# Four graph layers in one kernel: later layers' loads spread out, rank-4 rows last in a score stage, and new order plans

## The reference

```python
# layer 0: 8 heads of width 32, mask, output projection, layer norm
scores = where(adj + eye > 0, q @ k.T / sqrt(32), -inf);  out = softmax(scores) @ v
x = layernorm(x + out @ Wo.T + bo) * gamma + beta
# layer 1: 8 heads, scores + a_i + c_j + log(adj + 1e-9), then x + out
# layer 2: one head: softmax(leaky_relu(q_i + k_j + (1 - adj) * -1e9)) @ (x @ W_fc) + x
# layer 3: as layer 0, with + log(max(adj, 1e-8)) in place of the mask
```

## Time and profile before

| | |
|---|---|
| median of 3 runs | 1794.17 us (1792.88 to 1796.88) |
| profiled execution: its time, its span | 1796.79 us, 1795.0 us |
| mean granted TensorE clock | 0.991 |
| busy share PE, PE weight loads, DVE, ACT, POOL | 94%, 72%, 76%, 67%, 74% |
| HBM read and written | 62.93 MB, 8.39 MB |

### The profile page before, as it was taken

One profiled execution on the slowest core, in us unless ns is written; L12 is line 12 of the kernel. 1 busy time (PEld: TensorE's weight loads), 2 busy tenths in 40 slices (PEclk: granted clock), 3 DMA queues, 4 the chain that ended last, 5 costly groups with the idle time before them and its releaser, 6 DMA issues.

```text
span 1795.0 us, 53987 instructions
## 1 busy us (share of the span) xinstructions
PE 1684.0 (94%) x23308; PEld 1290.8 (72%) x23308; DVE 1371.3 (76%) x2556; ACT 1203.0 (67%) x1886; POOL 1330.2 (74%) x994
## 2 busy tenths in 40 slices
PE   4899999899999999889999999989999999998996
PEld 3677776787776777677777677767777777766874
DVE  2899777767699976776779987776778998777674
ACT  2567875467877786456877787546687778754675
POOL 3555799278977499638987759945898767992788
PEclk8999999999999999999999999999999999999998
DMA  7100010102121001100222100010123200101001
GB/s 217 43 19 19 16 29 25 36 14 66 55 89 49 18 15 37 31 19 19 74 82 66 37 19 20 27 47 7 31 73 94 61 19 14 32 25 36 14 26 42
DMA packets 76432, 74.79 MB, mean 42 GB/s; under 512 B 6562, under 2 KB 76196, under 8 KB 76196
## 3 DMA queue, kind: packets, MB, share of 16 engines
q1 hardware_dynamic: 75092, 70.55, 13.2%
q10 hardware_dynamic: 1104, 0.79, 0.1%
HBM read 62.93 MB, written 8.39 MB: 40 GB/s over the span
## 4 chain that ended last, share of the span: by engine, by line
PE 78%; DVE 9%; POOL 5%; ACT 3%; issue 3%; SPq 2%; DMA 1%; DVEq 0%; POOLq 0%; ACTq 0%
PE gx L640 23%; PE sc L738 18%; PE od L780 17%; PE gx L792 6%; PE sc L744 3%; PE sc L732 3%; PE gx L828 3%; PE gx L665 2%; ACT ring L906 1%; DVE negm L999 1%; PE gx L758 1%; DVE xs L1088 1%; DVE lg L1070 1%; DVE parts L999 1%; POOL xs L632 1%
## 5 line engine op out<-in xcount | busy, mean ns | idle before, releaser
L625 POOL TENSOR_TENSOR ring<-ring,adj_c 128x1024 f32<-128x1024 f32 x256 | 605.4, 2397 | 11.1 <-ACT ring L906 8.7
L738 PE MATMUL sc<-qk 32*128 32x256 f32 x9216 | 410.5, 294 | 31.2 <-DVE negm L999 11.1
L738 PEld LDWEIGHTS sc<-qk 32*128 32x128 f32 x9216 | 320.5, 184 | 135.6 <-issue 76.2
L888 ACT ACTIVATE aside<-sc 128x1024 f32<-128x1024 f32 x192 | 196.7, 1024 | 166.2 <-PE sc L738 113.3
L906 ACT ACTIVATE ring<-sc 128x1024 f32<-128x1024 f32 x256 | 248.3, 1023 | 49.9 <-PE sc L744 49.4
L780 PE MATMUL od<-ring,vf 128*32 128x256 f32 x3072 | 243.3, 388 | 7.0 <-issue 5.0
L780 PE MATMUL od<-ring,halves 128*32 128x256 f32 x3072 | 237.3, 380 | 0.0
L999 DVE TENSOR_REDUCE parts<-sc 128x4 f32<-128x1024 f32 x128 | 156.6, 1223 | 98.3 <-PE sc L738 96.8
L598 POOL TENSOR_TENSOR xs<-xs,bo 128x512 f32<-128x512 f32 x96 | 128.8, 1342 | 120.5 <-DVE xt_lo L969 120.1
L1026 DVE TENSOR_TENSOR ring<-ring,adj_c 128x1024 f32<-128x1024 f32 x128 | 182.2, 1464 | 0.0
L1002 DVE TENSOR_REDUCE parts<-aside 128x4 f32<-128x1024 f32 x128 | 154.9, 1211 | 16.7 <-ACT aside L888 16.5
(11 more groups left out here) (144 smaller groups left out, 4231.2 us busy)
## 6 DMA issues: line engine op xcount, KB each, us to landing
adj_c<-in_adj_t SPq DMA_DIRECT2D x96, 256.0 KB, 2.8
adj_r<-in_adj SPq DMA_DIRECT2D x64, 256.0 KB, 3.0
x_raw<-in_x_t SPq DMA_DIRECT2D x32, 256.0 KB, 3.4
xs<-in_x SPq DMA_DIRECT2D x32, 256.0 KB, 3.3
out<-xs SPq DMA_DIRECT2D x32, 256.0 KB, 2.2
wo<-in_w_o SPq DMA_DIRECT2D x2, 256.0 KB
ring<-in_w_q ACTq DMA_DIRECT2D x1, 256.0 KB, 3.8
ring<-in_w_k ACTq DMA_DIRECT2D x1, 256.0 KB, 5.1
```

The lines of the kernel that those rows point to most:

```text
L625: pool.tensor_tensor(part, part, adj_c[i.mi % 3][:, t, :].unsqueeze(1).to_broadcast([P, G, N]), ALU.mult).then_inc(weighted, 1)
L738: mm = pe.matmul(sc[:, g, t * N:(t + 1) * N], buf[rows, a, c, t * P:(t + 1) * P], buf[rows, b, c, :], start=(n == 0 and not masked), stop= ...
L888: act.activation(aside[:], sc[:, 0:2, :], ACT.Copy).then_inc(set_aside, 1)
```

## The change

Five things are changed.

1. At the start SP issues adj of item 1 early, adj transposed of item 0 ahead of x, and x of items 0 and 1 alone. The other loads of the first group go where their LX, LR and LC stages stand in SP's order. The 14 small transfers and the 7 weights go a few at a time behind LR.3 to LR.7. SPLIT_AT moves the splits of these weights later.
2. In a half of S or E, the 24 products of both blocks t come first, and the 8 products of `m_rows` or `c_rows` last. The wait for these rows moves behind the 24 products. Only the first product of a bank has the start flag.
3. In layer 0's S, the mask products wait only for the mask, and the wait for q and k comes behind them.
4. On POOL, the scaling of q's bias moves from ahead of the loop to behind T.0; the scaling of the biases of layers 1 and 3 moves from PC.5 to PC.7.
5. All plan places and the pitches are new numbers.

```diff
-SPLIT_AT = (None, -0.06, -0.05, 13, 15.2, 17.4, 19.6, 21.8, 24, 26.2)
+SPLIT_AT = (None, -0.06, -0.05, 19, 21, 23, 27, 33, 37, 41)
...
-    "S": {PE: [5.649, 6.16], ACTE: [6.962, 8.435], DVE: [6.511, 7.353]},
+    "S": {PE: [3.017, 5.338], ACTE: [5.417, 6.963], DVE: [4.727, 6.83]},
...
-    "A": {PE: [14.601, 15.151, 16.002, 16.487]},
+    "A": {PE: [13.593, 15.277, 15.581, 15.629]},
...
-    "E": {PE: [9.469, 11.767], ACTE: [11.406, 12.866], POOL: [1.816, 2.912], DVE: [12.575, 16.68]},
-    "A": {PE: [15.565, 15.586, 16.838, 16.969]},
+    "E": {PE: [8.072, 10.461], ACTE: [10.807, 12.327], POOL: [-6.299, -5.344], DVE: [2.323, 5.591]},
+    "A": {PE: [13.92, 14.286, 15.186, 15.196]},
...
-PITCH = {0: (4.4, 4.65), 1: (4.55, 4.45), 2: (4.65, 4.4), 3: (4.9, 4.95)}
+PITCH = {0: (4.6, 4.65), 1: (4.55, 4.55), 2: (4.75, 4.7), 3: (4.95, 4.9)}
...
+            sp.dma_start(adj_r[1][:], adj_all[rows_of[1].batch]).then_inc(adjr_loaded[1], 16)
             for dst, src in fold_plain:
                 sp.dma_start(dst, src).then_inc(w_fold, 16)
-            for i in items_l0[:GROUP]:
+            sp.dma_start(adj_c[0][:], adj_t_all[mha[0].batch]).then_inc(adjc_loaded[0], 16)
+            for i in items_l0[:2]:
                 sp.dma_start(xs[:, i.slot], x_all[i.batch]).then_inc(x_loaded[i.slot], 16)
...
-            for dst, src in plain:
-                sp.dma_start(dst, src).then_inc(w_plain, 16)
-            for n in range(3, len(WEIGHTS)):
-                load_weight(n)
+            def some_later_loads(n):
+                for dst, src in plain[6 * n:6 * n + 6]:
+                    sp.dma_start(dst, src).then_inc(w_plain, 16)
+                if n >= 2:
+                    for m in range(3, len(WEIGHTS))[3 * (n - 2):3 * (n - 1)]:
+                        load_weight(m)
...
+                    if 3 <= i.ar < GROUP:
+                        some_later_loads(i.ar - 3)
...
-            pool.wait_ge(w_first, 32)
-            pool.tensor_scalar(b_col["q0"][:], b_col["q0"][:], SCALE, None, ALU.mult).then_inc(cols_set, 1)
...
+                    if i.k == 0:
+                        pool.wait_ge(w_first, 32)
+                        pool.tensor_scalar(b_col["q0"][:], b_col["q0"][:], SCALE, None, ALU.mult).then_inc(cols_set, 1)
...
-                    if c == 0:
-                        if s == "S":
-                            pe.wait_ge(qk_lo_set, 4 * i.mi + 4)
-                            if i.l == 0:
-                                pe.wait_ge(mask_r_set, i.i0 + 1)
-                            if i.l == 1:
-                                pe.wait_ge(c_set, i.i1 + 1)
-                        else:
-                            pe.wait_ge(m_set, i.mi + 1)
...
-                        if extra is not None:
+                    if extra is not None:
+
+                        if c == 0:
+                            if s == "S":
+                                pe.wait_ge(c_set, i.i1 + 1)
+                            else:
+                                pe.wait_ge(m_set, i.mi + 1)
+                        for t in range(T):
                             for g in range(G):
```

More of the change, by code:

```diff
@@ L72 @@
-    "A": {PE: [14.601, 15.151, 16.002, 16.487]},
[L73 to L78, removed]
+    "O": {PE: [1.438], ACTE: [3.649], POOL: [-5.383]},
+    "T": {PE: [-4.035], ACTE: [-2.229], DVE: [-2.359]},
+    "Q": {PE: [-1.726], ACTE: [0.972], DVE: [0.299]},
+    "P": {PE: [-1.297], ACTE: [1.062], DVE: [0.516]},
+    "V": {PE: [0.406], ACTE: [2.076], DVE: [96.525]},
+    "S": {PE: [3.017, 5.338], ACTE: [5.417, 6.963], DVE: [4.727, 6.83]},
@@ L79 @@
+    "U": {DVE: [7.669]},
+    "M": {PE: [6.711], ACTE: [9.416]},
+    "E": {PE: [9.03, 10.762], ACTE: [10.388, 13.272], POOL: [4.746, 6.815], DVE: [15.191, 18.748]},
+    "A": {PE: [13.593, 15.277, 15.581, 15.629]},
+    "N": {DVE: [17.555]},
+    "F": {PE: [19.617]},
+    "XB": {POOL: [-7.724]},
+    "H": {DVE: [20.491]},
+    "LC": {SP: [44.42]},
+    "PC": {POOL: [-2.071]},
 }
 MHA_PLAN3 = {
-    "T": {PE: [-6.128], ACTE: [-5.034], DVE: [-6.002]},
-    "Q": {PE: [-0.869], ACTE: [0.837], DVE: [-0.372]},
@@ L94 @@
-    "LC": {SP: [22.274]},
-    "PC": {POOL: [-8.955]},
+    "T": {PE: [-6.107], ACTE: [-3.304], DVE: [-4.058]},
+    "Q": {PE: [-2.126], ACTE: [0.858], DVE: [0.342]},
+    "P": {PE: [0.592], ACTE: [1.918], DVE: [1.811]},
+    "V": {PE: [0.99], ACTE: [3.205], DVE: [63.745]},
+    "S": {PE: [2.413, 5.408], ACTE: [5.042, 6.794], DVE: [3.811, 6.542]},
+    "U": {DVE: [7.247]},
+    "M": {PE: [7.245], ACTE: [9.928]},
+    "E": {PE: [8.072, 10.461], ACTE: [10.807, 12.327], POOL: [-6.299, -5.344], DVE: [2.323, 5.591]},
@@ L96 @@
+    "A": {PE: [13.92, 14.286, 15.186, 15.196]},
+    "N": {DVE: [18.138]},
+    "F": {PE: [22.254]},
+    "XB": {POOL: [-17.948]},
+    "H": {DVE: [24.89]},
+    "LC": {SP: [24.223]},
+    "PC": {POOL: [-15.21]},
 }
 LN_PLAN0 = {
-    "B": {DVE: [23.449]},
-    "Z": {ACTE: [27.077]},
-    "Y": {DVE: [26.124], ACTE: [29.319], POOL: [27.197]},
+    "B": {DVE: [23.655]},
+    "Z": {ACTE: [26.241]},
+    "Y": {DVE: [26.25], ACTE: [27.932], POOL: [21.459]},
 }
 LN_PLAN3 = {
-    "B": {DVE: [27.746]},
@@ L104 @@
-    "Z": {ACTE: [31.23]},
-    "Y": {DVE: [30.39], ACTE: [34.223], POOL: [24.809]},
+    "B": {DVE: [25.008]},
+    "Z": {ACTE: [29.699]},
+    "Y": {DVE: [29.765], ACTE: [31.356], POOL: [17.541]},
 }
 FIRST_PLAN = {
[L108 to L111, removed]
+    "LT": {SP: [12.581]},
+    "LX": {SP: [33.723]},
+    "LR": {SP: [16.812]},
+    "PR": {POOL: [-19.152]},
 }
 LAST_PLAN = {
-    "OUT": {SP: [61.449]},
+    "OUT": {SP: [62.32]},
@@ L115 @@
 }
 GAT_PLAN = {
[L117 to L124, removed]
-    "LR": {SP: [29.847]},
-    "PR": {POOL: [-7.166]},
+    "T": {PE: [-6.852], ACTE: [-4.101], DVE: [-4.465]},
+    "G": {PE: [-3.965, -0.755], DVE: [-2.968, 1.37]},
+    "J": {ACTE: [1.804]},
@@ L127 @@
+    "K": {PE: [5.971]},
+    "L": {DVE: [8.022]},
+    "X": {ACTE: [11.185]},
+    "W": {PE: [11.789], ACTE: [14.078]},
+    "C": {DVE: [15.008], PE: [12.88]},
+    "LR": {SP: [28.845]},
+    "PR": {POOL: [-11.907]},
 }
-PITCH = {0: (4.4, 4.65), 1: (4.55, 4.45), 2: (4.65, 4.4), 3: (4.9, 4.95)}
+PITCH = {0: (4.6, 4.65), 1: (4.55, 4.55), 2: (4.75, 4.7), 3: (4.95, 4.9)}
 GAT_START, LAST_START = 23, 31
```

96 lines of the change are left out of this document (42 added, 54 removed).

## The result

The changed kernel takes 1787.87 us (median of 9 runs, 1784.17 to 1791.53), the kernel before 1795.74 us beside it. The ratio is 0.9963, 95% interval 0.9952 to 0.9973: faster by some 0.4%, 6 us slower than forecast. Against the kernel before beside it, it gains 7.9 us; 12.2 were forecast (1794.17 to 1782). The profiled execution has a time of 1789.48 us and a span of 1787.4 us.

A forecast was written before the change was run, and what follows sets the result against it. PE, busy 94% of the span, was taken as the bound, with about 125 us of waits. From 1796.8: -18.5 - 2 - 0.6 + 3.7 + 5 = 1784.4; the median is 2.6 lower: 1782 us, range 1764 to 1798.

The forecast's parts named there:

- The start, -18.5: First layer's start: E0.0 would start at 32.4 us in place of 50.94, saving 18.5 us, bounds -14 to -20.5.
- a wait inside the stage breaks the stream: Rival, chance 0.04: row products in E0 and S0 pay 0.1 us behind each wait, 13 us in all, giving 1795.
- The spread splits, -2: DVE from 60 to 100 us: weight splits spread over twice the stretch save 2 us, between 0 and -4.
- The clock at the start: New start stays at 2.4 GHz; if not, P.1 and S1.0 take 1.3 and 1.2 us more, losing 2.5.
- The body, +6.1: Everything behind the start: PE's new order -0.6, waits for `sc` +3.7, waits for `gx` +5, spread splits -2.
- +3.7 for `sc`: PE's waits for the single buffer `sc` between S and E halves, summed over layers 1, 3 and 0: +3.7 us.
- +5 for `gx`: PE's waits for the two `gx` buffers, almost all in layer 2: 37 to 42 us, so +5.
- Layer 1's term: More work between S1 and E1 in layer 1: waits for `sc` go from 15.2 to 3.7 us, -11.5.
- Layer 3's was +8.6: Less work between E1 and S0 in layer 3: waits for `sc` go from 8.7 to 17.3 us, +8.6.
- Layer 0's was +6.7: S and E halves next to each other in layer 0: waits for `sc` go from 2.9 to 9.6 us, +6.7.
- POOL sets layer 3's pace: Rival, chance 0.16: in layer 3, A3 waits for POOL, 1 us in 24 items, giving 1806 us.
- The body gains as well: Rival, chance 0.22: layer 1's 11.5 us come, layer 3's 8.6 and half the `gx` term go, giving 1768 us.

The follow-up runs named there:

- start_only: The kernel before with only the start's part of the change (SP's order, SPLIT_AT, POOL's bias steps): 1777.75 us, ratio 0.9903; again 1779.54 us.
- early_x: The kernel before with only x transposed of items 2 and 3 issued earlier on SP, ahead of the small loads and later weights: 1777.51 us, ratio 0.9901.
- rows_last_only: The kernel before with only the new form of a score stage, parts 2 and 3 of the change: 1793.92 us, ratio 0.9991.
- new_plans_old_stage: The changed kernel with the old form of a score stage, all waits first: 1789.20 us, ratio 0.9966.
- start_old_splits: start_only with the later weights' splits and POOL's scaling of the later biases back at their old places: 1776.83 us, ratio 0.9900.
- early_y: The changed kernel with Y.32, Y.64 and Y.96 on POOL moved ahead of PC and XB, PE's order unchanged: 1775.82 us, ratio 0.9887; again 1773.61 us.
- both: early_y with T.40, T.72 and T.104 also placed 0.6 units later on PE, ACT and DVE: 1777.71 us, ratio 0.9892.
- late_t: The changed kernel with T of layer 1's first slot 0.6 units later on PE, ACT and DVE in every group: 1777.33 us, ratio 0.9902.

## Why the prediction was partly wrong

**The start, -18.5: right.** E0.0 at 32.85 (forecast 32.4), behind `pick`; start_only, the spread splits among it, gives 17.6 us. The cause was narrower than the change: one late load (early_x).

**Rows last and mask first, 0: right** (rows_last_only, new_plans_old_stage). The rival that a wait inside the stage breaks the stream is refuted.

**The spread splits, -2: wrong**, no gain (start_old_splits). The busy share of one window, 60 to 100 us, said that the splits are in the way there; it did not say that they are less so further on.

**The clock at the start: right for P.1 and S1.0.** From 18 to 30.5 us the granted clock is 1.00, as the sum had it, and PE did not idle there. That is also what the Trainium skill's "TensorE: Matmul & The Clock Gate", section "Why this matters for your kernels", has: it is the long idle gap between bursts that puts PE back to half clock. The sum left out what comes next: PE idles 2.35 us ahead of E0.0, and from 32.8 to 37.0 us the clock is 0.57 to 0.61, which makes the 0.91 of the window. E0.0 to E1.0 takes 7.46 us in place of 6.63 before, so 0.8 us. That wait alone does not decide it: behind the same wait (2.36 and 2.34 us) early_y and both kept 1.00, late_t fell to 0.61 to 0.63.

**The body, +6.1 (-0.6 + 3.7 + 5 - 2): this is the step that failed**: it took every input of a stage as ready, so the wait of T for POOL's layer norm stood at nothing. It failed twice, in opposite directions. From E1.0 to E1.127 the body takes 9.4 us more than before (40.3 to 1761.5, in place of 57.6 to 1769.4). early_y's body takes 16.4 us less than the changed kernel's (39.2 to 1744.0), so 7.0 less than before's:

- *Left out:* the wait of T.40, T.72 and T.104 for Y on POOL, +16.4 us in these profiles, +12 to +14 by the medians. I had counted only what each pair of neighbours on PE shares, `sc` and `gx`, and taken each input as ready. The one input that comes down the other engines from the layer before was not: T.40 would have started 1.5 us after P.39 in place of 6.1, and its input was there after 5.1. 10.6 us of it are in the list of waits, 5.4 are the slower stretches behind them (below).
- *Over-priced:* the terms of +3.7 for `sc` and +5 for `gx`, where the cured order gives -7.0 in these profiles and -2 to -6 by the medians of the two pairs. Some 5 of the 7.0 lie behind E1.71, in stretches in which two runs of the old order differ by as much as 2.3 us (286.2 and 283.9 from E1.103 on, in before and rows_last_only); by a whole group, E1.39 to E1.71, it is -0.1, where the terms make +2. Layer 1's term was -11.5; seven items took 1.5 us less, which is 7 us for the layer's 32. The list of waits has 11.1 us of them before and 3.6 after, where the sum had 15.2 and 3.7. Layer 3's was +8.6, and the wait came: M to S0 takes 0.3 us more per item, 2.1 of the 2.8 us by which seven items grew (after the change one more pair of A2 and A3 lies in that stretch, 1.7 us, and other stages give 1 back). The stretch behind it, into layer 0, got 1.0 us shorter with T cured. Layer 0's was +6.7; that same stretch is shorter than before. Layer 2, with most of the +5: E1.15 to E1.24 went from 72.8 to 72.2, no loss at all. Where in layers 0 and 2 the summed waits were made up for stays open.

The failed step in the prediction's words: "everything else lies in the new order", followed by a sum over `sc` and `gx` alone. Its two errors, +12 to +16 missing and some 8 to 13 too much, cancelled in large part; that the total was only 6 us off is luck. 1.6 of these 6 us are no error of the sum: the kernel before took 1795.74 us this time in place of 1794.17.

**The rivals.** "POOL sets layer 3's pace" did not happen: PE's waits for POOL's `ring` are 4.1 us in sum. "The body gains as well" is, by its direction, what the changed kernel would have done without T's wait: 1775.8 measured, 1768 forecast. Its sum takes off 5 us as half of the `gx` term, which is the whole of it; with half it would be 1771. Its ground, that layer 3's waits cost nothing, was not shown. POOL did cost PE time, but in layer 0 and by the layer norm, where I had not looked.

## What to carry to other kernels

When an order on one engine is changed, check each moved stage against when its inputs are ready on the *other* engines, not only against the buffers it shares with its neighbours; a stage that moves a few microseconds forward can use up all its slack. A wait that is new or has grown is the first thing to look for in the list of waits after, by releaser: here one row with three entries held 10.6 us, and the loss with it. And before a start is rebuilt, move only the load that the chain names: two issues gave as much as the whole new loading scheme.

## What the runs showed of the hardware

A wait of 3.45 us on PE costs more than it lasts. The windows of the changed kernel before T.40, in its wait, behind it, and later (the last three columns: granted clock, DMA share, GB/s):

```profile
549.00:556.80 7.80, 7.63 (x114) 5.69 (x112) 7.66 (x14) 4.93 (x8) 7.71 (x6) 1.00 0.01 3
556.80:560.20 3.40, 0.01 (x1) 0.00 (x0) 3.07 (x4) 0.84 (x2) 3.32 (x2) 0.78 0.03 2
560.20:564.60 4.40, 4.12 (x32) 2.65 (x33) 0.69 (x1) 0.60 (x1) 2.64 (x4) 0.50 0.20 58
564.60:567.00 2.40, 2.40 (x16) 1.82 (x12) 2.28 (x2) 2.27 (x2) 2.40 (x3) 0.81 0.00 0
567.00:575.00 8.00, 7.93 (x117) 6.10 (x118) 7.82 (x14) 5.64 (x9) 4.83 (x4) 1.00 0.01 2
```

The clock was full, fell while PE idled, and was at 0.50, the level of 1.2 GHz, for the 4.4 us behind. From T.40 to E1.37 the changed kernel takes 6.71 us (560.26 to 566.97), early_y 4.23 (556.06 to 560.29): 2.5 us on top of the 3.45. Behind the waits of T.72 and T.104 the granted clock was 0.68 and 0.66 over the next 4.4 us, and the same stages took 5.60 and 5.81 us: 1.4 and 1.6 on top. The three waits, 10.6 us, and these 5.4 make 16.0, against 16.4 measured from E1.0 to E1.127.

The two POOL steps of Y.32 took 2.24 and 2.13 us, where the same two took 1.29 each in early_y. In the changed kernel they ran beside DVE's product of `ring` and `adj_c` (L1037, two in 4.29 us, where two took 2.99 in early_y); in early_y they ran mostly beside DVE's reductions and layer norm statistics. So each slowed the other, by 1.8 and 1.3 us. In early_y DVE's product ran beside a POOL step with one tensor input (L624) instead: that step took 2.78 us in place of 1.92, while the product had its 2.99. The Trainium skill's "SBUF — State Buffer", section "Who interferes with whom", names this pair (a DVE instruction with two inputs in SBUF and a GpSimd instruction that reads SBUF) and says that DVE reductions never contend; the trace agrees on both.
